# Two cross-attention layers: inputs passed in turned as well, layer-1 query and output products in split passes, row sums moved to VectorE

## The reference

```python
# layer 0: softmax over the 512 rows of x (axis 1), then residual and layer norm
q = x @ Wq + bq;  k = ctx @ Wk + bk;  v = ctx @ Wv + bv
w = softmax((q @ k.T) / 16, axis=1)
y = layernorm(w @ v + x) * gamma + beta
# layer 1: softmax over the 1601 rows of ctx (last axis), output projection, residual
Q = y @ Wq1 + bq1;  K = ctx @ Wk1 + bk1;  V = ctx @ Wv1 + bv1
out = y + softmax((Q @ K.T) / 16) @ V @ Wo + bo
```

## Time and profile before

| what | value |
|---|---|
| median of three runs | 467.65 us |
| span of the profiled execution | 464.6 us |
| TensorE busy | 443.7 us (96%) |
| ScalarE busy | 383.7 us (83%) |
| VectorE busy | 366.8 us (79%) |
| GpSimd busy | 365.0 us (79%) |
| DMA queue of SyncE, share of 16 engines | 11.8% |

### The profile page before, as it was taken

One profiled execution on the slowest core, in us unless ns is written; L12 is line 12 of the kernel. 1 busy time (PEld: TensorE's weight loads), 2 busy tenths in 40 slices (PEclk: granted clock), 3 DMA queues, 4 the chain that ended last, 5 costly groups with the idle time before them and its releaser, 6 DMA issues.

```text
span 464.6 us, 7967 instructions
## 1 busy us (share of the span) xinstructions
PE 443.7 (96%) x2433; PEld 371.6 (80%) x2433; DVE 366.8 (79%) x898; ACT 383.7 (83%) x819; POOL 365.0 (79%) x321
## 2 busy tenths in 40 slices
PE   8798899999999999999999999999999999799796
PEld 8686667887888888888888878888888878687596
DVE  3798978788886988778787888779877887578774
ACT  4899889987999789987899879987899879872473
POOL 0567699979999799887999789987999699963400
PEclk9999999999999999999999999999999999999999
DMA  9400200021100210020200210001100010000001
GB/s 262 130 24 24 71 24 2 23 72 34 36 23 1 72 47 23 24 55 18 70 23 1 71 49 23 24 18 55 46 1 0 3 46 1 0 0 25 23 1 45
DMA packets 23896, 17.29 MB, mean 37 GB/s; under 512 B 1055, under 2 KB 23854, under 8 KB 23854
## 3 DMA queue, kind: packets, MB, share of 16 engines
q1 hardware_dynamic: 23706, 16.66, 11.8%
q10 hardware_dynamic: 148, 0.13, 0.1%
HBM read 12.59 MB, written 4.19 MB: 36 GB/s over the span
## 4 chain that ended last, share of the span: by engine, by line
PE 79%; ACT 8%; DVE 5%; POOL 4%; issue 4%; DVEq 0%; POOLq 0%; ACTq 0%
PE ps_l L654 11%; PE ps_l L655 10%; PE ps_l L656 9%; PE ps_s L800 9%; PE ps_s L654 8%; PE ps_s L656 8%; PE ps_s L655 8%; ACT p L1048 3%; PE ps_s L774 3%; PE ps_s L841 3%; DVE max L1257 2%; POOL wsum L1376 2%; PE ps_l L687 2%; ACT p L1001 2%; PE ps_s L768 2%
## 5 line engine op out<-in xcount | busy, mean ns | idle before, releaser
L1376 POOL TENSOR_TENSOR wsum<-wsum,p 128x512 f32<-128x512 f32 (+1 forms) x88 | 116.3, 1322 | 13.4 <-ACT p L1007 11.8
L1383 POOL TENSOR_TENSOR p_lo<-p,p_hi 128x512 fp32r<-128x512 f32 (+1 forms) x91 | 117.2, 1295 | 2.6 <-ACT p_hi L1015 2.4
L1001 ACT ACTIVATE p<-s_sb,min 128x512 f32<-128x512 f32 (+1 forms) x104 | 75.4, 726 | 7.5 <-DVE min L1171 5.3
L1171 DVE CUSTOM_DVE_ANT_0 s_sb<-ps_l,cb 128x512 f32<-128x512 f32 (+1 forms) x104 | 70.4, 685 | 13.3 <-ACT p L1001 5.5
L1007 ACT ACTIVATE p<-p,r 128x512 f32<-128x512 f32 (+1 forms) x104 | 74.9, 728 | 1.4 <-DVE r L1178 1.3
L1192 DVE TENSOR_TENSOR p1T_lo<-ps_s,p1T_hi 128x512 fp32r<-128x512 f32 (+1 forms) x91 | 60.6, 683 | 14.4 <-ACT p1T_hi L1056 13.9
L1257 DVE TENSOR_REDUCE max<-ps_s 128x1 f32<-128x804 f32 x58 | 57.1, 992 | 10.0 <-PE ps_s L656 8.6
L1056 ACT CAST p1T_hi<-ps_s 128x512 fp32r<-128x512 f32 (+1 forms) x91 | 52.0, 586 | 14.9 <-PE ps_s L800 12.1
L1015 ACT CAST p_hi<-p 128x512 fp32r<-128x512 f32 (+1 forms) x104 | 63.5, 624 | 0.5 <-PE ps_l L656 0.4
L1048 ACT ACTIVATE p<-ps_s,bias 128x1206 f32<-128x1206 f32 (+1 forms) x58 | 53.6, 927 | 3.6 <-DVE bias L1268 3.1
L800 PE MATMUL ps_s<-ident,p 128*128 128x128 f32 (+1 forms) x364 | 49.6, 273 | 1.5 <-ACT p L1048 1.5
...
## 6 DMA issues: line engine op xcount, KB each, us to landing
ctx_sb<-in_ctx_dram SPq DMA_DIRECT2D x24, 256.0 KB, 2.9
...
out_dram<-y_res SPq DMA_DIRECT2D x16, 256.0 KB, 2.2
p<-in_L_xattn_Wq_dram SPq DMA_DIRECT2D x2, 256.0 KB, 4.2
...
p<-in_L_xattn_Wo_dram SPq DMA_DIRECT2D x1, 256.0 KB, 4.7
...
```

Source lines behind the costliest of these rows:

```text
L1001: nc.scalar.activation(p0[0:m, ring0(i), :], s0_sb[0:m, (a + i) % 2, :], ACT.Exp, bias=min0[0:m, i:i + 1], scale=-1.0, accum_out=sum0[0:m, ...
L1171: nc.vector.tensor_tensor_reduce(out=s0_sb[0:m, (a + i) % 2, :], in0=ps_s0[0:m, (a + i) % 2, :], in1=cb[a % 2][0:m, :], scale=-SCALE, scal ...
L1376: nc.gpsimd.tensor_tensor(total, total, p0[0:m, ring0(i), :], ALU.add).then_inc(wsum_done, 1)
L1383: nc.gpsimd.tensor_tensor(p0_lo[0:m, h, :], p0[0:m, ring0(i), :], p0_hi[0:m, h, :].bitcast(F32), ALU.subtract).then_inc(p0_lo_done, 1)
```

## The change

The host passes x, ctx and the weights Wq, Wk (both layers) and Wv (layer 1) turned as well, and the bias and scale vectors as columns. With that

- `turn_x`, `x_turned`, `xT_low`, `turn_ctx`, `turn_wq`, `turn_wk`, `turn_vectors`, `turn_w1` and `repeat` go; xT, ctxT, wqT, wkT and wvT are loaded by DMA;
- `project_q0` becomes a plain fp32 product of a0 and xT; `project_q1` and `project_out` become split products of three passes, with the new steps `xh_low`, `at1_low` and `at1_low_half` on VectorE;
- the row sums of both biases (`weigh_u0`, `sum_z0`, `weigh_u1`, `bias_row1`, `row_bias1`) become multiply-and-sum instructions on VectorE (`row_bias0`, `bias_row1`), four of 256 elements each;
- `sum_rows0` becomes four transposes and a reduction in `bias_x0`;
- ctx, ctxT and xT have one SBUF buffer, x keeps two; a load waits for the last reader of the batch before;
- all four engines' lists are written anew.

```diff
             def project_q0(a, _):
-                pe.wait_ge(xT_lo_done, EC * (a + 1))
+                pe.wait_ge(xT_loaded, 16 * (a + 1))
...
-                    mm = split3(ps_misc[:], a0_hi[:, c, :], a0_lo[:, c, :], xT_hi[:, c, :], xT_lo[:, c, :],
-                                start=(c == 0), stop=(c == EC - 1))
+                    mm = nc.tensor.matmul(ps_misc[:], a0_sb[:, c, :], xT_sb[:, c, :], start=(c == 0), stop=(c == EC - 1))
             def project_q1(b, _):
-                pe.wait_ge(xhT_done, EC * (b + 1))
+                pe.wait_ge(xhT_lo_done, EC * (b + 1))
...
-                    mm = nc.tensor.matmul(ps_q1, a1_gamma[:, c, :], xhT[:, c, :], start=(c == 0), stop=(c == EC - 1))
+                    mm = split3(ps_q1, a1g_hi[:, c, :], a1g_lo[:, c, :], xhT_hi[:, c, :], xhT_lo[:, c, :], start=(c == 0),
+                                stop=(c == EC - 1))
             def project_out(b, h):
...
-                    mm = nc.tensor.matmul(out_bank(b, h)[:, k * E:(k + 1) * E], at1[:, t], w2_sb[:], start=True, stop=True)
+                    mm = split3(out_bank(b, h)[:, k * E:(k + 1) * E], at1_hi[:, t], at1_lo[:, t], w2_hi[:], w2_lo[:])
             def sum_rows0(a, _):
...
-                    mm = nc.tensor.matmul(ps_misc[:, t:t + 1], wsum[a % 2][:, t * P:(t + 1) * P], ones[:, 0:1],
-                                          start=True, stop=True)
+                    mm = nc.tensor.transpose(ps_misc[:, t * P:(t + 1) * P], wsum[a % 2][:, t * P:(t + 1) * P], ident[:])
+            def row_bias0(a, _):
...
+                for t in range(TB):
+                    nc.vector.tensor_tensor_reduce(out=xr[:, t, :], in0=x_sb[a % 2][:, t, :], in1=u0_row[:], scale=1.0, scalar=0.0,
+                                                   op0=ALU.mult, op1=ALU.add, accum_out=z0[:, t:t + 1]).then_inc(z0_done, 1)
             def bias_x0(a, _):
...
-                nc.vector.tensor_copy(rowsum0[:], ps_misc[:, 0:TB]).then_inc(rowsum_done, 1)
+                nc.vector.tensor_reduce(rowsum0[:], ps_misc[:].rearrange("p (t m) -> p t m", m=P), AX_X, ALU.add
+                                        ).then_inc(rowsum_done, 1)
+            def xh_low(b, c):
+                dve.wait_ge(xhT_done, EC * b + c + 1)
+                nc.vector.tensor_tensor(xhT_lo[:, c, :], ps_y[c], xhT_hi[:, c, :].bitcast(F32), ALU.subtract
+                                        ).then_inc(xhT_lo_done, 1)
+            def at1_low(b, _):
+                dve.wait_ge(at1_done, b + 1)
+                nc.vector.tensor_tensor(at1_lo[:], ps_acc1, at1_hi[:].bitcast(F32), ALU.subtract).then_inc(at1_lo_done, 1)
             def ctxT_low(a, g):
...
-                nc.vector.tensor_tensor(ctxT_lo[a % 2][:, lo:hi], ctx_bank(a, g)[:, 0:hi - lo],
+                nc.vector.tensor_tensor(ctxT_lo[a % 2][:, lo:hi], ctxT_sb[:, lo:hi],
                                         ctxT_hi[a % 2][:, lo:hi].bitcast(F32), ALU.subtract).then_inc(ctxT_lo_done, 1)
```

More of the change, by code:

```diff
@@ L321, with xattn_kernel @@
 WARM = 10
-def xattn_kernel(nc, x, ctx, wq0, bq0, wk0, bk0, wv0, bv0, gamma, beta,
-                 wq1, bq1, wk1, bk1, wv1, bv1, wo, bo, out):
+def xattn_kernel(nc, x, xT, ctx, ctxT, wqT0, wkT0, wqT1, wkT1, wvT1, columns, wv0, bv0, gamma, beta, wo, bo, out):
     B, T, E = x.shape
@@ L422, in xattn_kernel @@
         u1_gamma = sb("u1_gamma", [P, E])
-        w2_sb = sb("w2_sb", [P, E])
+        w2_hi, w2_lo = (sb(f"w2_{part}", [P, E], F32R) for part in ("hi", "lo"))
         betaob_row = sb("betaob_row", [P, E])
@@ L663, in misc_free @@
                     was, n, k = misc_user.pop()
-                    if was == "turn_x":
-                        pe.wait_ge(xT_lo_done, EC * n + k + 1)
-                    elif was == "project_q0":
+                    if was == "project_q0":
                         pe.wait_ge(qw0_lo_done, n + 1)
@@ L871, in make_a, with row_of @@
                 return mm
+            def row_of(ps, col, rows_in):
+                for h in range(EC):
+                    mm = nc.tensor.matmul(ps, col[:, h:h + 1].broadcast_to([P, P]), rows_in[:, h, :],
+                                          start=(h == 0), stop=(h == EC - 1))
+                return mm
             def keep_warm(n):
@@ L929, in pre0 @@
                 keep_warm(WARM)
-                pe.wait_ge(w_loaded[0], 16)
-                turn_wq(0, s1_bank(0))
-                pe.wait_ge(wk0_loaded, 16)
-                turn_wk(0, s1_bank(1)).then_inc(wT_turned, 1)
-                turn_vectors(0, ps_acc0)
-                turn_x(0, 0)
-                turn_x(0, 1)
-                pe.wait_ge(wT_copied, 2)
-                make_a(0, s1_bank(2)).then_inc(made_ps, 1)
-                pe.wait_ge(reps_done, EC)
-                for h in range(EC):
-                    mm = nc.tensor.matmul(s1_bank(0)[:, 0:E], bk_rep[0][:, h, :], wqT[0][:, h, :],
-                                          start=(h == 0), stop=(h == EC - 1))
-                mm.then_inc(made_ps, 1)
-                turn_ctx(0, 0)
-                for h in range(EC):
-                    nc.tensor.matmul(ps_acc0[:, 0:1], wkT[0][:, h, :], bq_col[0][:, h:h + 1],
-                                     start=(h == 0), stop=(h == EC - 1))
-                for h in range(EC):
-                    mm = nc.tensor.matmul(ps_acc0[:, 1:2], bk_rep[0][:, h, :], bq_col[0][:, h:h + 1],
-                                          start=(h == 0), stop=(h == EC - 1))
-                mm.then_inc(small_ps, 1)
             steps = {f.__name__: f for f in (
-                turn_x, project_q0, project_bias0, turn_ctx, scores0, weigh0, sum_rows0, predict, turn_y, project_q1, scores1,
-                turn_p1, weigh1, turn_p1_half, weigh1_half, project_out, turn_w1, make_w1)}
+                project_q0, project_bias0, scores0, weigh0, sum_rows0, predict, turn_y, project_q1, scores1,
+                turn_p1, weigh1, turn_p1_half, weigh1_half, project_out, make_w0, make_w1)}
             pre0()
@@ new lines, in copy_w0 @@
+            def copy_w0(_, i):
+                if i == 0:
+                    act.wait_ge(a0_ps, 1)
+                    nc.scalar.copy(a0_sb[:].rearrange("p c l -> p (c l)"), s1_bank(2)[:, 0:E]).then_inc(a0_done, 1)
+                elif i == 1:
+                    act.wait_ge(u0_ps, 1)
+                    nc.scalar.copy(u0_row[:], s1_bank(0)[:, 0:E]).then_inc(u0_done, 1)
+                else:
+                    act.wait_ge(small_ps[0], 1)
+                    nc.scalar.copy(small[0][:], ps_acc0[:, 0:2]).then_inc(small_sb[0], 1)
@@ L1104, in pre0 @@
[L1104 to L1112 removed]
+                act.dma_start(wkT[0], wkT0.rearrange("(h p) l -> p h l", p=P)).then_inc(w_loaded[0], 16)
@@ L1350, in _ @@
             steps = {f.__name__: f for f in (
-                ctxT_low, xT_low, at0_low, bias_x0, q0_low, weigh_u0_first, sum_z0, max0, recip0, residual0, moments0, normalised, bias_row1,
-                q1_low, rowmax1, bias1_of, recip1, p0_low_first, p1_low, p1_low_half, finish, prepare_w1)}
+                ctxT_low, at0_low, bias_x0, q0_low, row_bias0, max0, recip0, residual0, moments0, normalised, xh_low, bias_row1,
+                q1_low, rowmax1, bias1_of, recip1, p0_low_first, p1_low, p1_low_half, at1_low, at1_low_half, finish, prepare_w1)}
             pre0()
@@ L1447 @@
     for name in _INS:
-        a = np.ascontiguousarray(inputs[name])
+        if name == "columns":
+            a = np.stack([inputs[n] for n in COLUMNS]).reshape(len(COLUMNS), -1, P).transpose(2, 1, 0)
+        elif name in TURNED:
+            a = np.swapaxes(inputs[TURNED[name]], -1, -2)
+        else:
+            a = inputs[name]
+        a = np.ascontiguousarray(a)
         arrays[f"in_{name}_dram"] = a
```

484 lines of the change are left out of this document (200 added, 284 removed), and 454 rows, old and new, of tables (GPSIMD_HEAD, GPSIMD_STEADY, SCALAR_HEAD, SCALAR_STEADY).

## The result

The changed kernel takes 514.99 us (median of four runs, 514.47 to 515.06) for 467.38 of the kernel before on the same chip: ratio 1.102, 95% interval 1.1005 to 1.1043. The forecast was 446.0, faster. The profiled span is 513.1 us for 464.6.

A forecast was written before the change was run, and what follows sets the result against it. TensorE was taken to bound steady batches, ScalarE the first batch's first layer. Start -1.9, first batch -2.3, steady part -18.2 and end +0.8 sum to -21.6: span 464.6 to 443.0, median of runs 446.0, range 440 to 451.

The forecast's parts named there:

- TensorE, -3.15 per batch: Sum of TensorE's removed transposes and changed products per batch: -3.15 us, leaving 50.0, all on the path in steady batches.
- A steady batch costs what TensorE's instructions cost: Steady batches: TensorE busy 52.84 of 53.1 us, idle only 0.26, so TensorE is the bound.
- Idle time added, 0.45 (0 to 0.9): Extra TensorE idle per steady batch from longer chains: 0.45 us, upper bound from the filling batch; net gain 2.7.
- twelve operations of this kind: VectorE operations with both inputs in SBUF, eight sums and four ctxT_low, disturbed by GpSimd: 12 x 0.11 = 1.3 us per batch.
- Rival 3: VectorE's two-SBUF operations wait out GpSimd instructions, making VectorE the bound at 52.6 us per batch: 461 us; chance 0.06.
- The median of 0.689 as evidence against: First-batch p_lo on VectorE took 0.689 us in the median, like an undisturbed one: used against full blocking by GpSimd.
- the trace agrees only in part: On the skill's rule that two-SBUF VectorE instructions and GpSimd exclude each other: median 0.689 us looked undisturbed, worst 1.128 not.
- Rival 4: VectorE keeps its 9.9 us of waits per batch, so a batch takes 57.2 us: 492 us, slower; chance 0.05.
- Loads: The added loads of transposed copies, one landing 2.9 us, stay covered in steady batches and cost nothing.
- Start: Up to the first scores0: a0 comes first without weight transposes, -1.9 us (0 to -2.5), first scores0 near 12.3.
- First batch, -2.3: First batch, bound by ScalarE, which loses copies of turned weights and x_turned: -2.3 us (0 to -3.5).
- End: Last batch's exposed at1_low_half and xh_low plus bias sums: +0.8 us (0 to +2).

The follow-up runs named there:

- b3: Kernel before, orders kept, with xT loaded from the second batch on and project_q0 plain fp32; turn_x, x_turned, xT_low gone: 464.9 us, ratio 0.9961.
- b7: Kernel before with xT loaded, split project_q1 and project_out, transposed row sums, GpSimd held for bias_x0, at1_low between normalised's halves: 490.0 us.
- b8: b7 with scores0 ahead of project_q1 on TensorE and both xh_low ahead of finish's second half on VectorE: 478.5 us, ratio 1.025.
- b9: b7 with project_q1 left a plain fp32 product, so without xh_low: 467.8 us, ratio 1.002.
- e6: e5 with bias_x0 taken off VectorE, its work done by TensorE products and by residual0 adding x: 490.1 us.
- e5: Changed kernel with bias_row1 directly behind normalised and GpSimd made to wait for bias_x0 and bias_row1: 490.3 us, ratio 1.0505.
- e4: Changed kernel with GpSimd's sum_weights and p0_low cut to 64 of 512 columns from the third batch on: 478.1 us, ratio 1.025.
- f1: Kernel before with row sums as multiply-and-sum on VectorE, both groups behind normalised, GpSimd held until they are done: 494.0 us, ratio 1.056.

## Why the prediction was wrong, point by point

- **TensorE, -3.15 per batch: right.** In the changed kernel the plain project_q0 takes 1.72 us from start to start, project_out's twelve passes 1.36, the four transposes of wsum 0.43, and project_q1 starts its six passes 0.23 apart.
- **"A steady batch costs what TensorE's instructions cost": too strong.** Busy time counts the overlapping tails of its instructions and hides small pauses. As an estimate I take the 25th percentile of the start-to-start distances of each kind of instruction as its undisturbed cost. By the kind of the instruction, or of it and the next, the work of a period is then 51.8 or 50.7 us of 53.3 before and 48.9 or 50.2 of 58.5 after: 1.5 to 2.6 us of pauses before, not 0.26, and 8 to 10 after. The rule itself nearly held where no step was added: b3, with 0.59 less to do, gained 0.5 us per period.
- **Idle time added, 0.45 (0 to 0.9): the failed term.** It measures 6 to 8 us per batch: 6.6 to 8.5 by TensorE's busy time, less the 0.26 of before, and 5.7 to 8.1 by the estimate above. "TensorE idles over 2 us in one", a sign to watch, came true. The bounds came from the batch in which the pipeline fills, which has the old steps at the old distances; it says nothing on what two more steps in the chain from xhat to scores1 cost. b7, b8 and b9 price xh_low alone, with the blocking of bias_x0 held off: 22 us with the old order, 11 with a better one, for 0.31 us per batch saved.
- **VectorE, "twelve operations of this kind" at 0.11: the failed term before it.** The kind was right, the price was not (1.0 us when it meets one), nor the count: the eight unchanged instructions of bias_x0 and normalised, and the copy-like tensor_scalar, are of it too. They showed no disturbance before because GpSimd stood waiting there or ran only its pow; 37.5 of 61.3 us of excess are theirs. VectorE's 47.3 became 52; the sign to watch, "busy over 49", came true.
- **Rival 3 named the mechanism** and gave 461. Its figure for VectorE, 52.6 us, was met (52), by luck in part: it has 6.6 us on twelve instructions, and in the window from 233.80 some 2.7 fell on those and 5.0 on bias_x0 and normalised. Its error was to let VectorE's busy time set the batch. The blocked instructions stand on the path from the last weigh0 to scores1, TensorE pauses for them, and its clock can fall behind a pause (in the first whole period after, 0.92).
- **The median of 0.689 as evidence against** The earlier trace rows misled, and "the trace agrees only in part" was a misreading: those p_lo come in the first batch, when GpSimd is 65% busy, and each of the 13 is long or not as a GpSimd instruction was running when it began, as shown above. The median shows only that most missed it. The question to ask of the trace was how often an instruction would begin beside GpSimd in the new orders.
- **Rival 4** (492) was nearest: VectorE did keep idle time (6.7 to 8.3 us of 58.5 to 59.9 for 9.9).
- **Loads: right** in steady batches; no load ends a wait there. **Start: right** (12.8 for 12.3). **First batch, -2.3: wrong**, it ends 5.9 later than expected, and 3 of its 4 bias_x0 instructions are blocked; without bias_x0 on VectorE (e6) it is 4 us shorter, and the rest stays open. **End: right** within 1 us.

How much of the 69 us is which: blocking with what follows from it, the half clock among it, is at least 25 (e5). e4 gives back 37, but it bounds nothing from above, as it leaves 26.3 us of excess, and GpSimd's own path is shorter in it too. For the rest, the orders with their longer chains, the evidence is from the old orders (b7 to b9, f1) and from TensorE's waits for xh_low in e5; in the new orders no run takes a step out alone, and that stays open.
